# Last mixture of experts in half-precision parts, token loop outermost, and fused norms ahead of and behind it

## The reference

```
def _L1_ffn_ref(x, Wq, bq, Wk, bk, Wv, bv, Wo, bo, g1, be1, g2, be2, Wg, bg, We, bexp):
    def layernorm(x, g, b):
        m = jnp.mean(x, axis=-1, keepdims=True)
        v = jnp.mean((x - m) ** 2, axis=-1, keepdims=True)
        return (x - m) * jax.lax.rsqrt(v + EPS) * g + b
    ...                                   # self-attention -> ctx
    attn_out = ctx @ Wo + bo
    x = x + layernorm(attn_out, g1, be1)
    gate_probs = jax.nn.softmax(x @ Wg + bg, axis=-1)
    top_vals, top_idx = jax.lax.top_k(gate_probs, TOP_K)
    all_out = jnp.einsum('bsd,edf->bsef', x, We) + bexp
    picked = jnp.take_along_axis(all_out, top_idx[..., None], axis=2)
    moe_out = jnp.sum(top_vals[..., None] * picked, axis=2)
    return x + layernorm(moe_out, g2, be2)
```

## Time and profile before

| | us |
|---|---|
| median of 3 executions | 1970.18 (1969.29 to 1971.75) |
| profiled execution | 1973.04 |
| its span (first to last instruction) | 1971.3 |
| PE busy in the span | 1693.7 (86%) |
| DVE busy | 1312.9 (67%) |
| ACT busy | 1077.4 (55%) |
| granted TensorE clock, mean | 0.916 of full |

### The profile page before, as it was taken

One profiled execution on the slowest core, in us unless ns is written; L12 is line 12 of the kernel. 1 busy time (PEld: TensorE's weight loads), 2 busy tenths in 40 slices (PEclk: granted clock), 3 DMA queues, 4 the chain that ended last, 5 costly groups with the idle time before them and its releaser, 6 DMA issues.

```text
span 1971.3 us, 34546 instructions
## 1 busy us (share of the span) xinstructions
PE 1693.7 (86%) x13836; PEld 921.8 (47%) x13836; DVE 1312.9 (67%) x1998; ACT 1077.4 (55%) x1928; POOL 274.9 (14%) x248
## 2 busy tenths in 40 slices
PE   6988868999789999846999999999999768986686
PEld 4556655666547888521333333333334323552342
DVE  4223344380456888659999999999982786239556
ACT  3312112887634887212999999999997025213410
POOL 3223002898230000300000000000000000000000
PEclk9989989999788999875999999999999879986878
DMA  8123011899533766165325325435200251044100
GB/s 317 65 86 101 23 44 32 288 293 291 186 112 102 241 223 205 51 115 99 59 61 92 82 59 91 85 59 86 55 25 2 50 66 44 1 79 54 44 0 21
DMA packets 144620, 196.60 MB, mean 100 GB/s; under 512 B 34422, under 2 KB 109832, under 8 KB 140200
## 3 DMA queue, kind: packets, MB, share of 16 engines
...
...
## 4 chain that ended last, share of the span: by engine, by line
PE 45%; DVE 39%; issue 5%; POOL 4%; DMA 3%; ACT 2%; SPq 1%; another core or an unknown queue 1%; DVEq 0%; POOLq 0%; ACTq 0%
DVE mx_part L2179 27%; PE bank L1184 5%; PE pair L1226 5%; DVE mx L2272 3%; PE pair L1553 3%; PE pair L1139 2%; PE bank L1037 2%; PE pair L1152 2%; DMA xT<-x_slots 2%; PE bank L249 2%; PE bank L1328 2%; PE pair L1387 2%; POOL k_part L2479 2%; PE bank L1081 2%; PE bank L1443 1%
## 5 line engine op out<-in xcount | busy, mean ns | idle before, releaser
L1730 ACT ACTIVATE pexp_all<-bank 128x512 f32<-128x512 f32 x1024 | 551.8, 596 | 98.0 <-PE bank L1342 84.4
L2179 DVE TENSOR_REDUCE mx_part<-pair 128x2 f32<-128x1024 f32 x512 | 583.1, 1216 | 16.5 <-PE pair L1314 14.1
L1328 PE MATMUL bank<-pexp_all,vst 128*17 128x256 f32 x4096 | 321.4, 386 | 6.0 <-issue 6.0
L1314 PE MATMUL pair<-kst,qs 49*128 49x512 f16 x1024 | 210.1, 407 | 44.6 <-DVE mx_part L2179 28.0
L1342 PE MATMUL bank<-qs,kst 52*128 52x256 f16 x2048 | 203.3, 271 | 0.0
L1314 PEld LDWEIGHTS pair<-kst,qs 49*128 49x128 f16 x1024 | 50.3, 93 | 273.2 <-DVE mx_part L2179 215.1
L1342 PEld LDWEIGHTS bank<-qs,kst 52*128 52x128 f16 x2048 | 120.8, 95 | 56.9 <-ACT pexp_all L1730 18.4
L1740 ACT ACTIVATE pexp_all<-bank 128x512 f32<-128x512 f32 x128 | 67.6, 595 | 121.9 <-PE bank L1450 121.8
L1328 PEld LDWEIGHTS bank<-pexp_all,vst 128*17 128x17 f32 x4096 | 68.6, 95 | 114.7 <-issue 105.3
L1664 ACT ACTIVATE hid_f<-bank,b 128x256 f32<-128x256 f32 (+1 forms) x152 | 78.6, 518 | 51.7 <-PE bank L1184 36.7
L1226 PE MATMUL pair<-w_hi,hid_hi 128*128 128x256 f16 x368 | 101.7, 276 | 4.0 <-issue 2.6
...
## 6 DMA issues: line engine op xcount, KB each, us to landing
w_f<-in_w_all SPq DMA_DIRECT2D x34, 1024.0 KB, 5.6
kst<-k_scr SPq DMA_DIRECT2D x192, 128.0 KB
...
ctx_sb<-in_ctx SPq DMA_DIRECT2D x16, 1024.0 KB, 5.0
...
k_scr<-k_part SPq DMA_DIRECT2D x128, 128.0 KB, 3.7
...
```

Source lines behind the costliest of these rows:

```text
L1314: last = pe.matmul(pair[n % 2][:, e * 512:(e + 1) * 512], qs[g % NBK][rws, p, qt * P:(qt + 1) * P], kst[g % NBK][rws, p, kb * 512:(kb + 1) ...
L1328: last = pe.matmul(bank[3][32 * h:32 * h + HV, 0:S], vst[g % 2][:, c, h * HV:(h + 1) * HV], unit_exp[n % NUE][:, p * S:(p + 1) * S], start ...
L1730: act.activation(unit_exp[n % NUE], bank[SCORE_BANKS[n % 3]], ACT.Exp, scale=SCALE).then_inc(s_exp, 1)
L2179: dve.tensor_reduce(mx_part[:, :, 2 * p + qt, kb], pair[n % 2][:, :].rearrange("p (e k) -> p e k", e=2), X_AXIS, ALU.max).then_inc(s_mx, 1)
```

## The change

- **Expert products**: in f16 parts. The turned tokens get a high part (a second destination of ACT's copies, `x6_part[0]`) and a low part (DVE, four subtractions). The weights get theirs in the second half of the last self-attention: eight conversions on ACT, one before every fourth exponential from number 32 on, and eight low parts on DVE, at odd steps from 17 on. The 2 MB load moves for that from behind the fourth batch of maxima rows to behind the second. 64 f32 matmuls become 192 in f16.
- **Order on PE**: tokens outermost. Tile 0 stands ahead of the wait for the gates, then the gate transposes, tile 1, the eight bias products (into banks 0 to 3, two tiles per bank), and tiles 2 to 7.
- **Order on DVE**: per tile eight accumulations, the first of which writes `tok`; the gates are divided by `W_SCALE` once. Bias and `bn_stats` of a tile come after the next tile's accumulations. The copies of the bias products are gone.
- **Norms**: `dve_rstd` has four steps instead of five, everywhere. `norm6a` is followed by two fused instructions per tile, (tok - mean) x g1 and x rstd + u, instead of a normalising pass, two passes and adds; the transposes wait for four tiles at a time, not for eight. The last norm is done in three groups of tiles (0 to 3, 4 to 6, 7), fused likewise, and each group is stored by its own DMA.
- **Bias adds** `be1` (now into `u`) and `be2` (into `x`) move into four steps (18, 20, 22, 24) of the last self-attention, two tiles at a time.

`dve_measure` in the diff is the part of `dve_norm` that aggregates the statistics and adds epsilon. The core of the diff:

```diff
+            r, q = rstd[:, lo:hi], rtmp[:, lo:hi]
...
-            st.link(dve.tensor_tensor(rtmp[:, :], rstd[:, :], rstd[:, :], ALU.mult))
+            st.link(dve.scalar_tensor_tensor(out=q, in0=r, scalar=-0.5, in1=r, op0=ALU.mult, op1=ALU.mult))
             st.settle()
-            st.link(dve.tensor_tensor(rtmp[:, :], rtmp[:, :], var_eps[:, :], ALU.mult))
+            st.link(dve.tensor_tensor(q, q, var_eps[:, lo:hi], ALU.mult))
             st.settle()
-            st.link(dve.tensor_scalar(rtmp[:, :], rtmp[:, :], -0.5, 1.5, ALU.mult, ALU.add))
+            st.link(dve.scalar_tensor_tensor(out=r, in0=q, scalar=1.5, in1=r, op0=ALU.add, op1=ALU.mult))
...
+        LAST_TILES = [(0, 4), (4, 7), (7, 8)]
...
-                sp.wait_ge(s_x, 6 * T)
-                sp.dma_start(out.rearrange("b (h p) d -> p (b h) d", p=P), x[:, :, :]).then_inc(s_store, 16)
-                sp.wait_ge(s_store, 16)
+                for lo, hi in LAST_TILES:
+                    sp.wait_ge(s_x, 5 * T + hi)
+                    sp.dma_start(out.rearrange("b (h p) d -> p (b h) d", p=P)[:, lo:hi, :], x[:, lo:hi, :]).then_inc(s_store, 16)
+                sp.wait_ge(s_store, 16 * len(LAST_TILES))
...
+                    if b == 1 and sa.turn == 1:
+                        sp.dma_start(l_we[:, :, :, :], a["l_we"].rearrange("e (k p) n -> p e k n", p=P)).then_inc(s_wa, 16)
...
-            pe_turn(pe, turn7, lambda half: pe.wait_ge(s_y6, T))
+            pe_turn(pe, turn7, lambda half: pe.wait_ge(s_y6, 4 * (half + 1)))
...
+            def expert_tile(t):
+                for e in range(ER // 2):
+                    n = ER // 2 * t + e
+                    if n >= 4:
+                        pe.wait_ge(s_wee, 2 * (n - 3))
+                    for k in range(KT):
+                        for i, (x_, w_) in enumerate(((0, 0), (1, 0), (0, 1))):
+                            last = pe.matmul(bank[4 + n % 4], x6_part[x_][:, k, t * P:(t + 1) * P], l_part[w_][:, e, k, :],
+                                             start=(k == 0 and i == 0), stop=(k == KT - 1 and i == 2))
+                    last.then_inc(s_we, 1)
+            pe.wait_ge(s_wlo, FIRST_PIECES + KT * ER // 2)
+            pe.wait_ge(s_xlo, FIRST_INPUTS + 4)
+            expert_tile(0)
...
+            expert_tile(1)
...
+                pe.matmul(bank[t // 2][:, D * (t % 2):D * (t % 2 + 1)], gateT[0:ER, t * P:(t + 1) * P], b2_l[:, :],
+                          start=True, stop=True, skip_group_check=True).then_inc(s_b2, 1)
+            for t in range(2, T):
+                expert_tile(t)
...
+                    if sa.turn == 1 and n >= 32 and n % 4 == 0:
+                        last_weights_high((n - 32) // 4)
...
+            def beside_last(n):
+                if n >= 17 and n % 2 == 1:
+                    last_weights_low((n - 17) // 2)
+                if n in (18, 20, 22, 24):
+                    i = (n - 18) // 2
+                    ts = slice(2 * i, 2 * i + 2)
+                    st.link(dve.tensor_tensor(u[:, ts, :], u[:, ts, :], per_tile_rows("L1_ffn_be1", 2), ALU.add))
+                    st.link(dve.tensor_tensor(x[:, ts, :], x[:, ts, :], per_tile_rows("L1_ffn_be2", 2), ALU.add))
...
+            dve_measure(dve, st, norm6a)
+            dve_rstd(dve, st, norm6a)
             for t in range(T):
-                dve.tensor_tensor(u[:, t, :], u[:, t, :], tok[:, t, :], ALU.add).then_inc(s_y6, 1)
+                st.link(dve.scalar_tensor_tensor(out=tok[:, t, :], in0=tok[:, t, :], scalar=meanvar[:, t, 0:1],
+                                                 in1=row("L1_ffn_g1"), op0=ALU.subtract, op1=ALU.mult))
+                st.settle()
+                dve.scalar_tensor_tensor(out=u[:, t, :], in0=tok[:, t, :], scalar=rstd[:, t:t + 1], in1=u[:, t, :],
+                                         op0=ALU.mult, op1=ALU.add).then_inc(s_y6, 1)
+            for half in range(2):
+                hs = slice(half * 512, (half + 1) * 512)
+                for k in range(KT):
+                    dve.wait_ge(s_tev, turn7.ev + 2 * (2 * half + k + 1))
+                    dve.tensor_tensor(x6_part[1][:, k, hs], xT[:, k, hs], x6_part[0][:, k, hs], ALU.subtract).then_inc(s_xlo, 1)
...
+            def accumulate(t):
+                for e in range(ER // 2):
+                    n = ER // 2 * t + e
                     dve.wait_ge(s_we, n + 1)
                     for j in range(2):
-                        if e or j:
-                            dve.wait_ge(s_wee, 2 * n + 1 if j else 2 * (n - T) + 2)
-                        dve.scalar_tensor_tensor(out=tok[:, t, :], in0=bank[4 + n % 4][:, j * D:(j + 1) * D],
-                                                 scalar=gate_t[:, t, 2 * e + j:2 * e + j + 1], in1=tok[:, t, :],
-                                                 op0=ALU.mult, op1=ALU.add).then_inc(s_wee, 1)
-                    if e == ER // 2 - 1 and t:
-                        dve.wait_ge(s_wee, 2 * n)
-                        tile_stats(dve, st, tok, t - 1)
-                    n += 1
-            dve.wait_ge(s_wee, ER * T)
-            tile_stats(dve, st, tok, T - 1)
-            dve_norm(dve, st, norm6m, tok, tok, measured=True)
-            st.link(dve.tensor_tensor(tok[:, :, :], tok[:, :, :], per_tile_rows("L1_ffn_g2"), ALU.mult))
-            st.settle()
-            for t in range(T):
-                dve.tensor_tensor(x[:, t, :], x[:, t, :], tok[:, t, :], ALU.add).then_inc(s_x, 1)
-            dve.wait_ge(s_x, 6 * T)
+                        src = bank[4 + n % 4][:, j * D:(j + 1) * D]
+                        gate = gate_s[:, t, 2 * e + j:2 * e + j + 1]
+                        if e == 0 and j == 0:
+                            dve.tensor_scalar(tok[:, t, :], src, gate, None, ALU.mult).then_inc(s_wee, 1)
+                        else:
+                            dve.wait_ge(s_wee, 2 * n + j)
+                            dve.scalar_tensor_tensor(out=tok[:, t, :], in0=src, scalar=gate, in1=tok[:, t, :],
+                                                     op0=ALU.mult, op1=ALU.add).then_inc(s_wee, 1)
+            def add_gated_bias(t):
+                dve.wait_ge(s_b2, 2 * (t // 2 + 1))
+                dve.wait_ge(s_wee, ER * (t + 1))
+                st.link(dve.tensor_tensor(tok[:, t, :], tok[:, t, :], bank[t // 2][:, D * (t % 2):D * (t % 2 + 1)], ALU.add))
+                st.settle()
+                tile_stats(dve, st, tok, t)
+            def last_norm(i):
+                lo, hi = LAST_TILES[i]
+                dve_rstd(dve, st, norm6m[i], lo, hi)
+                for t in range(lo, hi):
+                    st.link(dve.scalar_tensor_tensor(out=tok[:, t, :], in0=tok[:, t, :], scalar=meanvar[:, t, 0:1],
+                                                     in1=row("L1_ffn_g2"), op0=ALU.subtract, op1=ALU.mult))
+                    st.settle()
+                    dve.scalar_tensor_tensor(out=x[:, t, :], in0=tok[:, t, :], scalar=rstd[:, t:t + 1], in1=x[:, t, :],
+                                             op0=ALU.mult, op1=ALU.add).then_inc(s_x, 1)
+            accumulate(0)
+            for t in range(1, T):
+                accumulate(t)
+                if t == 5:
+                    last_norm(0)
+                add_gated_bias(t - 1)
+                if t - 1 == 3:
+                    dve_measure(dve, st, norm6m[0], *LAST_TILES[0])
+            dve_measure(dve, st, norm6m[1], *LAST_TILES[1])
+            add_gated_bias(T - 1)
+            dve_measure(dve, st, norm6m[2], *LAST_TILES[2])
+            last_norm(1)
+            last_norm(2)
```

85 lines of the change are left out of this document (35 added, 50 removed).

## The result

The changed kernel takes **1946.07 us** (median of 4 runs, 1943.5 to 1951.0) against 1970.97 (4 runs, 1969.29 to 1974.39) for the kernel before on the same chip: a ratio of 0.9871, with a 95% interval from 0.9855 to 0.9888. That is 24.9 us less; 1945.5 was forecast, 24.7 less.

The account below looks back on a forecast made before the run. PE was taken to bound the product stage, DVE the changed kernel from tile 5. From the last norms to the end 24.7 us less, self-attention +1.6, other norms -1.6: net 24.7 off 1970.18, 1945.5 us; range 1940 to 1951.

Parts of the forecast that it names:

- one pair of fused steps: Norm ahead of the router: two fused DVE instructions per tile, between 0.86 and 1.04 us, taken as 0.95.
- bias products: Eight bias matmuls on PE behind tile 1, at 0.43 us each: 3.4 us, ending at 1898.9.
- from there to DVE's start on tile 5: Product stage, from the end of the bias products until DVE starts tile 5 at 1917.1: 18.2 us.
- DVE alone: From tile 5 to the last add DVE is the bound: accumulations, bias, statistics and three norm groups, 26.8 us.
- store and rest: End of the kernel: last 128 KB store 2.3 us plus 0.4 at the end, 2.7 in all.
- added to a group of self-attention: Second half of self-attention: PE's next product waits for the copy behind DVE's low part, 0.15 us per group.
- self-attention in all: Conversions added under the last self-attention: 8 x 0.15 and 0.4 at the last, +1.6 us, bounds 0 and 4.3.
- DVE over 95% busy: Confirming sign at the end of the kernel: DVE busy more than 95% of the time from tile 5.
- The first rival: Granted clock falls again: at the bias products 1.9 us, at tile 7 DVE delayed 3.4; about 1950; chance 0.15.
- Wrong if the clock reads 0.50 in tiles 2 to 7: Refuting sign in the expert products: a granted clock of 0.50 (1.2 GHz) in these tiles would show the forecast wrong.
- The other norms: Eight norms elsewhere on the path each lose a root step of 0.20: -1.6 us, bounds 0 and -1.9.
- Rivals 2 to 5: PE at half clock, 0.03; self-attention pays fully, 0.12; better than assumed, 0.07; late parts or no visible change, 0.03.

Follow-up runs that it names:

- the second: The trace of the changed kernel run once more, nothing edited against the changed kernel: 1928.98 us against 1952.32 for the kernel before, ratio 0.9884.

## Why the prediction was right

Each step as the prediction put it, with what the first trace of the changed kernel shows:

| step | predicted | measured |
|---|---|---|
| inverse root, four steps | 0.84 | 0.84 (1857.88 to 1858.72) |
| one pair of fused steps | 0.95 | 0.92 (1859.24 to 1865.66, seven pairs) |
| all sixteen | 7.7 | 7.44 |
| last fused step to all turned | 3.4 | 3.3 |
| router | 7.0 | 6.99 |
| tile 0 | 7.1 | 6.76 |
| gate transposes, tile 1 | 1.0, 5.2 | 0.87, 5.18 |
| bias products | 3.4 | 3.65 |
| from there to DVE's start on tile 5 | 18.2 | 19.8 |
| DVE alone | 26.8 | 26.85 |
| store and rest | 2.7 | 2.2 |
| **reciprocal to end** | **83.5** | **83.9** |
| added to a group of self-attention | 0.15 | 0.10 (2.58 against 2.48) |
| self-attention in all | +1.6 | +1.05 by the groups; +3.1 in this trace, +2.4 in the second |

**What bounds.** PE was the bound of the product stage, and half precision with the 0.216 us of the shared expert's rows was the right price: tile 1's 24 matmuls took 5.18 us, and 72 of them 17.35 of which some 1.8 are the clock. The Trainium skill (TensorE: Matmul & The Clock Gate, section "Back-to-back issue gap") gives about 131 ns for such a matmul in a stream with weight loads; every dense tile here disagrees, at 216.

**One price was misread.** The bias products were put at half of 0.86 us each, by the earlier trace rows. The row there is 7.27 us for eight, 0.91 each; half of it gives 3.6, and 3.65 was measured against the 3.4 forecast.

**What changed hands.** From tile 5 on DVE is the bound, for 26.85 us against 26.8. The experiments that moved work off it shortened the end, to 80.30 and then 75.91 us behind the norm. The prediction's sign for it, DVE over 95% busy, did not come (91%); that no row waits for PE is the better sign.

**The first rival came true in part.** It was given 0.15 and about 1950. The clock did fall at both places. Behind the bias products the fall cost 1.6 to 1.8 us, as priced (1.9). Ahead of tile 7 it cost nothing. The prediction's 3.4 us for it let all 24 matmuls of the tile run at half clock; eight did, from 1923.97 to 1927.35, and DVE, which reached the tile at 1927.25, found each product in time, the last by 0.24 us. So the rival's event came without most of its price: the total from the norm to the end moved by 0.4 only, because tile 0, the fused steps and the store came out better by 0.3, 0.3 and 0.5. The time was right by steps that were right, and also by luck: small errors of both signs cancel. "Wrong if the clock reads 0.50 in tiles 2 to 7" was one of the prediction's own signs, and for 3.3 us each in tiles 2 and 7 it did. The Trainium skill (TensorE: Matmul & The Clock Gate, section "A second HAM failure mode: psum-queue depth-cycling") describes a clock that swings when matmul groups wait for banks again and again. This trace has only one such wait, ahead of tile 7 (2.66 us, then 0.50), so it neither confirms nor refutes that; the earlier trace rows, on which the rival stood, are at 0.50 throughout and do not swing. The fall behind the bias products is another case: PE shows no wait there at all.

**Self-attention.** The sum had the right owners and one size too large. ScalarE's conversion fits, as said, and so do DVE's bias adds between the copy and the reciprocal, within 0.1 us in all; the low part ahead of the copy is what stretches the group, as said, by 0.08 to 0.10 instead of 0.15 (half precision alone has it without the adds). The last step came out as put (0.37 against 0.4). The term is 1.05, not 1.6. What the sum had no term for lies outside the groups: against the kernel before, the first trace has 1.6 us more ahead of the copy at step 16 and 0.4 behind the last copy, the second 0.2 and 1.2. The 1.6 did not repeat; that stretch took 83.6 to 88.4 us across the traces, 85.5 and 84.8 in two kernels without the conversions. The part behind the last copy goes with the granted clock behind the gather (17.1 us at 0.72, 17.5 at 0.60, 18.2 to 18.3 at 0.50); whether the change moves that clock is not shown.

**The other norms.** 1.6 us were forecast for eight shorter roots. Each is 0.21 shorter, but the experiment with them alone gives 1.001; its interval excludes the 2.1 us of all eleven, and 1.6 less is its very edge. This term is not confirmed. The median came out right with it, within an interval of 3 us either way, so it does not vouch for terms of this size.

**Rivals 2 to 5.** The clock did not stay at half, self-attention's groups did not pay fully, no product was faster than its rows, and the parts did not come late.
